# Moving the drive's scaling from TensorE matmuls to GpSimd, and five VectorE steps with it, in a selective-scan block

## The reference, cut to what matters

```python
h   = layernorm(x)                                   # residual of the block
xz  = h @ W_in + b_in;  x_in, z = split(xz)          # 2 x 256 channels
xc  = silu(causal_conv4(x_in) + conv_b)
B, C = split(xc @ W_xp + b_xp)                       # 16 states each, per token
delta = softplus(xc @ W_dt + b_dt)
for s in range(16):                                  # scan over the 256 tokens
    state[s] = exp(delta * A[s]) * state[s] + (delta * xc) * B[s]   # "drive" = u * B[s]
    y += state[s] * C[s]
y   = (y + D_skip * xc) * silu(z)                    # "gate"
r   = h + y @ W_out + b_out
r   = alpha * (r - mean(r)) / (std(r) + eps) + beta  # "alpha, beta"
x1  = x + layernorm(r)                               # "residual sum"
x2  = x1 + layernorm(fp8(layernorm(x1)) @ fp8(W).T + bias)
```

## Time and profile before

| | us |
|---|---|
| runs: median (lowest to highest) | 679.10 (677.97 to 680.75) |
| the profiled execution's own time | 680.76 |
| its span | 679.0 |
| busy in the span: TensorE, VectorE, ScalarE, GpSimd | 559.0, 576.2, 416.4, 322.5 |
| mean granted TensorE clock | 0.909 of full |

### The profile page before, as it was taken

One profiled execution on the slowest core, in us unless ns is written; L12 is line 12 of the kernel. 1 busy time (PEld: TensorE's weight loads), 2 busy tenths in 40 slices (PEclk: granted clock), 3 DMA queues, 4 the chain that ended last, 5 costly groups with the idle time before them and its releaser, 6 DMA issues.

```text
span 679.0 us, 10276 instructions
## 1 busy us (share of the span) xinstructions
PE 559.0 (82%) x2893; PEld 429.9 (63%) x2893; DVE 576.2 (85%) x1106; ACT 416.4 (61%) x814; POOL 322.5 (47%) x331
## 2 busy tenths in 40 slices
PE   4889999997999799986999699979997887773371
PEld 3467787775777577775777567767776776662120
DVE  4057898899998989899989998999989998985595
ACT  2447875785667757776478457765777654621364
POOL 3033554545555536455454654553655545431264
PEclk7979999997999899998999799989999899987555
DMA  7000000000000000000000000000000000000012
GB/s 208 9 1 1 0 1 1 1 0 1 1 1 1 0 2 0 0 0 0 0 0 0 0 1 0 0 0 0 0 0 0 1 1 0 1 1 0 0 47 77
DMA packets 9959, 6.20 MB, mean 9 GB/s; under 512 B 2624, under 2 KB 8896, under 8 KB 9920
## 3 DMA queue, kind: packets, MB, share of 16 engines
q1 hardware_dynamic: 9920, 5.78, 3.1%
HBM read 3.68 MB, written 2.10 MB: 9 GB/s over the span
## 4 chain that ended last, share of the span: by engine, by line
PE 42%; DVE 33%; issue 14%; ACT 5%; POOL 4%; DVEq 1%; DMA 0%; POOLq 0%; ACTq 0%
PE drive L951 16%; DVE state L1162 12%; PE hT L967 8%; PE fbank L894 7%; DVE acc_d L1185 4%; PE fbank L910 2%; PE bbank L985 2%; DVE delta L1145 2%; DVE acc_d L1182 2%; DVE yv L1191 1%; PE drive L894 1%; DVE yg L1196 1%; DVE bst L1205 1%; POOL state L592 1%; ACT h L622 1%
## 5 line engine op out<-in xcount | busy, mean ns | idle before, releaser
L1162 DVE TENSOR_TENSOR_SCAN state<-decay,drive 128x512 f32<-128x512 f32 x256 | 297.1, 1201 | 19.4 <-PE drive L951 18.2
L951 PE MATMUL drive<-diag,uT 128*128 128x256 f32 x1024 | 253.4, 392 | 1.6 <-DVE state L1162 1.0
L951 PEld LDWEIGHTS drive<-diag,uT 128*128 128x128 f32 x1024 | 193.2, 199 | 29.1 <-issue 3.3
L711 ACT ACTIVATE decay<-delta,a_neg 128x510 f32<-128x510 f32 x256 | 169.5, 723 | 20.3 <-DVE state L1162 19.2
L967 PE MATMUL hT<-ident,state 128*128 128x128 f32 x1024 | 147.4, 284 | 36.6 <-DVE acc_d L1185 35.3
L967 PEld LDWEIGHTS hT<-ident,state 128*128 128x128 f32 x1024 | 122.6, 147 | 67.5 <-issue 51.6
L729 ACT ACTIVATE term<-hT,Ct 128x256 f32<-128x256 f32 x256 | 102.6, 478 | 55.3 <-PE hT L967 55.3
L497 POOL TENSOR_SCALAR_AFFINE_SELECT diag<-Bt 128x512 f32<-128x512 f32 x128 | 98.1, 776 | 61.4 <-PE drive L951 40.8
L1185 DVE SCALAR_TENSOR_TENSOR acc_d<-hT,Ct,acc_d 128x256 f32<-128x256 f32 x224 | 92.2, 467 | 0.9 <-PE hT L967 0.9
L512 POOL TENSOR_TENSOR acc<-acc,term 128x512 f32<-128x512 f32 x48 | 61.1, 1272 | 46.6 <-ACT term L729 46.6
L527 POOL TENSOR_TENSOR bstd<-bvar,minus_half 128x4 f32<-128x4 f32 x16 | 16.3, 1017 | 107.2 <-DVE bvar L1253 62.6
(11 more groups left out here) (165 smaller groups left out, 613.3 us busy)
## 6 DMA issues: line engine op xcount, KB each, us to landing
out_dram<-state SPq DMA_DIRECT2D x8, 256.0 KB, 2.2
x_all<-in_L_attn_x_dram SPq DMA_DIRECT2D x2, 256.0 KB, 4.5
state<-in_L_attn_conv_w_dram SPq DMA_DIRECT2D x1, 512.0 KB, 5.8
w_in<-in_L_attn_W_in_dram SPq DMA_DIRECT2D x1, 256.0 KB, 3.1
w_dt<-in_L_attn_W_dt_dram SPq DMA_DIRECT2D x1, 256.0 KB, 5.0
w_out<-in_L_attn_W_out_dram SPq DMA_DIRECT2D x1, 128.0 KB, 3.5
w_ffn<-in_L_ffn_weight_dram SPq DMA_DIRECT2D x1, 64.0 KB, 2.6
bout_r<-in_L_attn_b_out_dram SPq DMA_DIRECT2D x1, 64.0 KB, 3.3
```

Source lines behind the costliest of these rows:

```text
L711: last = nc.scalar.activation(decay[:, g % DECAYS, h, :, s, 1:], delta[:, par, h, :, 1:], ACT.Exp, scale=a_neg[:, h, SG * g + s:SG * g + s ...
L951: last = nc.tensor.matmul(dst[:, :, P * c:P * c + P], uT[:, par, TC * b + c, P * h:P * h + P], diag[:, n % DIAGS, c, :, :], start=True, st ...
L1162: nc.vector.tensor_tensor_scan(state[:, n % STATES, h, :, :].rearrange("p s t -> p (s t)"), decay[:, g % DECAYS, h, b, :, :].rearrange("p ...
```

## The change

The drive is made another way: GpSimd scales the token-major `uT` by B, one tensor_scalar of 128x256 for each chunk and state with B as a scalar for each partition (`scale_b`), into `scaled`; TensorE then only transposes it, eight 128x128 transposes a unit. `front_u`, `back_gate`, alpha and beta, and the residual sum go from VectorE to GpSimd (for the last pair they stay on VectorE); `back_h2T` goes to ScalarE. `TERMS` goes from 4 to 2, `LAG_A` from 3 to 4, and the four step tables are new.

```diff
-LAG_T, LAG_C, LAG_A = 2, 3, 3
+LAG_T, LAG_C, LAG_A = 2, 3, 4
-DECAYS, DIAGS, STATES, TERMS = 2, 4, 4, 4
+DECAYS, SCALED, STATES, TERMS = 2, 4, 4, 2
-POOL_STEPS = dict(front_root=(0,), front_residual=(19,), sum_states=(8,), back_root=(15, 21, 26))
-ACT_STEPS = dict(front_xin=(5, 10), silu_table=(21,), front_silu=(21, 22, 23), exp_table=(23,),
-                 front_norm=(16,), front_xnT=(23,), front_dt=(29, 30), front_exp=(35,), front_log=(35,),
-                 front_uT=(42, 46), back_norms=(33, 41, 47))
-PE_STEPS = dict(front_in=(3, 6, 15, 21), front_transpose=(23,), front_dt=(24, 29), front_bc=(36,),
-                front_ut=(40, 42), back_y=(14, 17), back_out=(20,), back_transpose=(46,))
-DVE_STEPS = dict(front_stats=(1,), front_shift=(2,), front_low=(21,), front_bc=(25,), front_delta=(24,),
-                 front_u=(25,), back_y=(9, 11), back_gate=(11,), back_norms=(11, 13, 17, 21, 24, 27, 27),
-                 back_amax=(30,), back_h2T=(31,))
+POOL_STEPS = dict(front_root=(1,), front_residual=(13,), front_u=(23,), back_gate=(10,), back_affine=(20,),
+                  back_sum=(23,), sum_states=(4,), back_root=(14, 22, 26))
+ACT_STEPS = dict(back_h2T=(47,), front_xin=(8, 12), silu_table=(21,), front_silu=(21, 22, 23), exp_table=(23,),
+                 front_norm=(19,), front_xnT=(23,), front_dt=(29, 33), front_exp=(34,), front_log=(36,),
+                 front_uT=(44, 44), back_norms=(33, 42, 47))
+PE_STEPS = dict(front_in=(0, 5, 16, 19), front_transpose=(22,), front_dt=(24, 28), front_bc=(32,),
+                front_ut=(38, 41), back_y=(14, 15), back_out=(18,), back_transpose=(47,))
+DVE_STEPS = dict(front_stats=(0,), front_shift=(1,), front_low=(19,), front_bc=(21,), front_delta=(23,),
+                 back_y=(9, 10), back_norms=(13, 13, 15, 21, 23, 27, 28), back_amax=(31,))
...
-            def diag_b(pr, par, n):
+            def scale_b(pr, par, n):
                 g, b = n // PAIR, n % PAIR
                 if n == 0:
                     pool.wait_ge(bc_ready, nth(pr, 3, 2))
+                    pool.wait_ge(uT_ready, nth(pr, 2, 2))
-                old = trailing(pr, par, n, DIAGS)
+                old = trailing(pr, par, n, SCALED)
                 if old:
                     pool.wait_ge(drive_ready, nth(old[0], 2 * UNITS, 2 * old[2] + 2))
...
-                nc.gpsimd.affine_select(out=diag[:, n % DIAGS, :, :, :].rearrange("p c s t -> p (c s) t"), in_=b_cols,
-                                        compare_op=ALU.is_equal, fill=0.0, base=0, pattern=[[0, TC * SG], [-1, P]],
-                                        channel_multiplier=1).then_inc(diag_ready, 1)
+                for c in range(TC):
+                    for s in range(SG):
+                        last = nc.gpsimd.tensor_scalar(scaled[:, n % SCALED, c, s, :], uT[:, par, TC * b + c, :],
+                                                       Bt[:, par, g, b, c, s:s + 1], None, ALU.mult)
+                last.then_inc(scaled_ready, 1)
...
+            def front_u(pr, par):
+                pool.wait_ge(delta_ready, nth(pr, 1, 1))
+                nc.gpsimd.tensor_tensor(u[:, :, :], d, xc[:, par, :, :], ALU.mult).then_inc(u_ready, 1)
+            def back_gate(pr, par):
+                pool.wait_ge(y_ready, nth(pr, 2, 2))
+                nc.gpsimd.tensor_tensor(yg[:, :, :], yv[:, :, :], sz[:, par, :, :], ALU.mult).then_inc(gated, 1)
+            def back_affine(pr):
+                pool.wait_ge(b_normed, nth(pr, 2, 1))
+                nc.gpsimd.tensor_tensor(chunks(nrm[:, :]), chunks(nrm[:, :]), on_chunks(alpha_r[:, :]), ALU.mult)\
+                    .then_inc(b_affine, 1)
+                pool.wait_ge(b_affine, nth(pr, 2, 1))
+                nc.gpsimd.tensor_tensor(chunks(nrm[:, :]), chunks(nrm[:, :]), on_chunks(beta_r[:, :]), ALU.add)\
+                    .then_inc(b_affine, 1)
+            def back_sum(pr):
+                pool.wait_ge(b_normed, nth(pr, 2, 2))
+                nc.gpsimd.tensor_tensor(x1, x1, nrm[:, :], ALU.add).then_inc(b_sum, 1)
...
             def drive_unit(pr, par, n):
-                if n == 0:
-                    pe.wait_ge(uT_ready, nth(pr, 2, 2))
-                pe.wait_ge(diag_ready, nth(pr, UNITS, n + 1))
+                pe.wait_ge(scaled_ready, nth(pr, UNITS, n + 1))
...
                     for c in range(TC):
-                        last = nc.tensor.matmul(dst[:, :, P * c:P * c + P], uT[:, par, TC * b + c, P * h:P * h + P],
-                                                diag[:, n % DIAGS, c, :, :], start=True, stop=True)
+                        for s in range(SG):
+                            last = nc.tensor.transpose(drive[:, n % 2, h, L * s + P * c:L * s + P * c + P],
+                                                       scaled[:, n % SCALED, c, s, P * h:P * h + P], ident[:, :])
...
+            def back_h2T(pr):                         # on ScalarE
+                act.wait_ge(back_full, nth(pr, 4, 4))
+                nc.scalar.activation(h2T[:, bass.ds(pr.v * TOK, TOK)], back_bank(pr, 3), ACT.Copy).then_inc(h2T_ready, 1)
```

More of the change, by code:

```diff
@@ L212, in build_sandwich @@
         decay = sb("decay", [P, DECAYS, HALVES, PAIR, SG, L])
-        diag = sb("diag", [P, DIAGS, TC, SG, P])
+        scaled = sb("scaled", [P, SCALED, TC, SG, DI])
         state = sb("state", [P, STATES, HALVES, SG, L])
@@ L328, in build_sandwich @@
         b_root = sem("b_root")
+        b_sum = sem("b_sum")
+        b_affine = sem("b_affine")
         b_shift = sem("b_shift")
@@ L537, in steps_at @@
                         front_residual(nxt, npar)
+                    for _ in due(POOL_STEPS, "front_u", at):
+                        front_u(nxt, npar)
                 if back:
@@ L540, in steps_at @@
                         sum_states(prv, ppar)
+                    for _ in due(POOL_STEPS, "back_gate", at):
+                        back_gate(prv, ppar)
+                    for _ in due(POOL_STEPS, "back_affine", at):
+                        back_affine(prv)
+                    for _ in due(POOL_STEPS, "back_sum", at):
+                        back_sum(prv)
                     for k in due(POOL_STEPS, "back_root", at):
@@ L546, in slot @@
                     if units == UNITS and n + LEAD < units:
-                        diag_b(pr, par, n + LEAD)
+                        scale_b(pr, par, n + LEAD)
                     elif front:
-                        diag_b(pr.plus(1), 1 - par, n + LEAD - units)
+                        scale_b(pr.plus(1), 1 - par, n + LEAD - units)
                     steps_at(pr, par, 2 * n, front, back)
@@ L574, in _ @@
             front_root(Pair(1))
+            front_residual(Pair(0), 0)
+            front_u(Pair(0), 0)
             for n in range(LEAD):
-                diag_b(Pair(0), 0, n)
-            front_residual(Pair(0), 0)
+                scale_b(Pair(0), 0, n)
             slot(Pair(0), 0, True, False)
@@ L696, in front_uT @@
                 act.wait_ge(front_full, nth(pr, 9, 8 + k))
+                if pr.after(2):
+                    act.wait_ge(scaled_ready, nth(pr.plus(-1), UNITS, 0))
                 nc.scalar.activation(uT[:, par, 2 * k:2 * k + 2, :],
@@ L763, in steps_at @@
                         back_norms(prv, k)
+                    for _ in due(ACT_STEPS, "back_h2T", at):
+                        back_h2T(prv)
             def slot(pr, par, front, back, units=UNITS):
@@ L1145, in front_delta @@
                 nc.vector.tensor_tensor(d, dt_v[:, :, :], dt_e[:, :, :], ALU.max).then_inc(delta_ready, 1)
-            def front_u(pr, par):
-                dve.wait_ge(delta_ready, nth(pr, 1, 1))
-                d = delta[:, par, :, :, :].rearrange("p h b t -> p h (b t)")
-                nc.vector.tensor_tensor(u[:, :, :], d, xc[:, par, :, :], ALU.mult).then_inc(u_ready, 1)
             def scan_half(pr, par, n, h):
@@ L1260, in back_sum @@
             def back_sum(pr, par):
[L1262 to L1265 removed]
+                if is_last(pr):
+                    dve.wait_ge(b_normed, nth(pr, 2, 2))
+                    x1 = x_all[:, bass.ds(pr.v * TOK, TOK)]
+                    nc.vector.tensor_tensor(x1, x1, nrm[:, :], ALU.add).then_inc(b_sum, 1)
+                dve.wait_ge(b_sum, nth(pr, 1, 1))
                 dve.sem_inc(dve_waited, 1)
[L1267 removed]
+                stats_of(pr, lambda j: x_all[:, bass.ds(pr.v * TOK + DM * j, DM)], 6)
                 nc.vector.tensor_scalar(bvar[:, :], bmv[:, :, 1], LN_EPS, None, ALU.add).then_inc(b_var, 1)
@@ L1302, in steps_at @@
                         front_delta(nxt, npar)
-                    for _ in due(DVE_STEPS, "front_u", at):
-                        front_u(nxt, npar)
                 if back:
@@ L1307, in steps_at @@
                         back_y(prv, ppar, h)
-                    for _ in due(DVE_STEPS, "back_gate", at):
-                        back_gate(prv, ppar)
                     for k in due(DVE_STEPS, "back_norms", at):
@@ L1313, in steps_at @@
                         back_amax(prv)
```

(3 more changed lines are left out.)

31 lines of the change are left out of this document (13 added, 18 removed).

## The result

The changed kernel takes 846.3 us in the median, against 678.5 before: a ratio of 1.246, with a 95% interval of 1.242 to 1.250. The forecast was 639 us, with 622 to 690 as its range. One run of four took 1119 us, far from the other three (845.5 to 846.8); nothing here explains it, and it is left out of this. The profiled execution took 846.8 us with a span of 844.9.

A forecast was written before the change was run, and what follows sets the result against it. VectorE bounds the kernel now; after the change GpSimd (62.6 us a slot) and VectorE (61.8) nearly tie. Savings 34 (six slots) + 6.5 (slot 0) + 4 (last slot) - 3 (prologue) = 41.5; 680.8 - 41.5 = 639.3, forecast 639, range 622 to 690.

The forecast's parts named there:

- T: Time of one 256-element tensor_scalar in GpSimd's scaling: taken as 0.45 us, from 0.26 to 0.75; 64 a slot make 28.8.
- GpSimd, the open price: Prediction's section on GpSimd's load a slot: 37.7 us today, 62.6 after the change, from 50.4 to 81.8.
- The rest of GpSimd's sum: GpSimd's slot load without scaling: 25.4 us left after losing diag, plus five moved elementwise steps, together 33.8 us.
- Rival 2: GpSimd's scaling dearer still, so TensorE and VectorE wait for `scaled`: slower, 726 us at 0.65 a piece, 775 at 0.75; chance 0.14.
- VectorE's sum: VectorE's busy time in a looped slot falls from 66.9 to 61.8 us, as 5.13 us of steps leave it.
- TensorE's: TensorE's busy time a slot falls from 64.5 to 50.9 us, a unit's drive from 1.89 to 1.04.
- The walk through a slot: One slot followed through all queues: closed at 65 us, plus 1.5 for meetings, 66.5 a slot.
- The ends of the program: Outside the looped slots: prologue 3 us more, last slot 4 less, tail unchanged.
- Rival 1: GpSimd's scaling piece costs 0.49 to 0.56 us and GpSimd is the bound, still faster: 654 to 677 us; chance 0.19.
- Rival 3: TensorE's clock stays down under transposes: 5 us more a slot, about 715 us; chance 0.03.
- Rival 4: u's handover through the engines before a slot's first drive ends 6 us late, gain gone: 679 us; chance 0.07.
- The lock between VectorE and GpSimd: Two-input SBUF instructions of VectorE exclude GpSimd's: some 3 us of waiting a slot inside VectorE's busy time, left unchanged.

The follow-up runs named there:

- half-scaled kernel: Changed kernel with only the first of a unit's two states scaled, the second slice filled with 0.5 once in the prologue; 648.5 us.
- moves alone: Changed kernel with the drive undone (diag by affine_select and matmuls as before), the moved steps and new step tables kept; 653.3 us, ratio 0.960 to the kernel before.
- copy kernel: Changed kernel with a GpSimd tensor_copy of 256 elements in place of each scaling tensor_scalar, B left out of the drive; 636.3 us.
- drive alone: Kernel before with only the drive changed (tensor_scalar scaling on GpSimd, transposes on TensorE) and two term buffers; elementwise steps and tables as before; 815.5 us.
- mixed kernel: Changed kernel with drives by turns: even units tensor_tensor scaling and transposes, odd units affine_select diag and matmuls; 652.4 us, ratio 0.959.

## Why the prediction was wrong, and where it was right

**The step that failed** is the price of T, in "GpSimd, the open price". It took T = 0.45 from affine_select, as the nearest one-input instruction, and 0.75 from the two-input adds as the upper bound. Measured: 0.93 (0.91 from start to start), so 64 of them are 58 us a slot where the sum had 28.8. Both ends rested on one idea, that the number of inputs sets GpSimd's rate. The runs show that the operation sets it: at 256 elements a copy takes 0.40, a tensor_scalar 0.86 with a constant and 0.93 with a scalar for each partition, and a tensor_tensor of 512 with a broadcast input 1.05, less than a tensor_scalar of 512 with 1.57. The bound "above" was no bound. The sentence "Against: there is only one input" put weight where there was none.

**The rest of GpSimd's sum** held. Its load without the scaling was put at 33.8 us; 91.5 less 64 x 0.907 is 33.4. Rival 2 named the mechanism and its place, and with 0.907 in its own formula gives 33.8 + 58.0 + 2.5 = 94.3 for the slot; it was 92.5. It had a chance of 0.14, and its price ended at T = 0.75 and 775 us, so 846 lay outside even that rival, in the 0.03 left for something slower still.

**VectorE's sum** held: 61.8 forecast, 62.0 measured. **TensorE's** held where the scaling did not hold it up: 1.04 us for a unit's drive at the full clock, and 52.4 us busy a slot in the half-scaled kernel for the 50.9 forecast. In the changed kernel it was 58, at the lower clock.

**The walk through a slot** held. With half the scaling, the slot was 67.1 for 66.5; with copies at 0.40, 65.9. That alpha and beta would be the tightest place shows in the half-scaled kernel, where VectorE waited 9.6 us for beta in six slots, the largest of its waits. GpSimd waited 2.1 us a slot for `delta` there, as walked. The stall at `back_res` came to 0.2 us in all six slots; the walk had left it 0.5 in each. Not as walked: scans waited for a drive up to 1.0 us, 7.5 in all in those six slots, where no wait over 0.3 was forecast.

**The ends of the program** were mis-sized. In the half-scaled kernel the span fell by 32.3: 30.6 in the six slots (forecast 34), 4.1 ahead of the first uT copy (forecast 3.5), and behind the last copy it rose by 2.4 where 4 less were forecast. Split at the end of the last scan, that last part is a last slot that fell by 1.6 and a tail that rose by 4.0, where the prediction had 4 less and "The tail is unchanged". In the moves alone the last slot fell by 4.5 and the tail rose by 3.3; in the copy kernel by 3.9 and 4.6. So the tail is what the prediction had wrong in all three, and in the half-scaled kernel the last slot as well. The gate comes 7.9 us behind the last scan in the kernel before, 11.5 in the half-scaled kernel and 11.1 with the moves alone.

It is not GpSimd's adds. The last of them ended at 573.6 in the half-scaled kernel, and VectorE took up the sum at 576.5, behind its own direct sums, which had waited for transposes of TensorE, and these for ScalarE:

```profile
568.89 0.60 ACT L776 ACTIVATE h2T<-bbank 128x512 f32<-128x512 f32 x1 [0.75 <-PE bbank L1040]
569.38 1.56 ACT L769 ACTIVATE term<-hT,Ct 128x256 f32<-128x256 f32 x4
570.36 1.76 PE L1011 MATMUL hT<-ident,state 128*128 128x128 f32 x8 [1.51 <-ACT term L769]
572.37 1.27 POOL L524 TENSOR_TENSOR acc<-acc,term 128x512 f32<-128x512 f32 x1
576.53 1.29 DVE L1423 TENSOR_TENSOR ysumT<-acc,acc_d 128x512 f32<-128x512 f32 x2
```

The term that TensorE waits for stands behind the moved `back_h2T`. Nor is it the later adds and two term buffers: with four buffers and the old distance the tail rose as well, by 4.5. That the place of `back_h2T` is the cause is read from these rows; no run undoes that move alone.

**Rival 1** (0.49 to 0.56, still faster) did not occur, though the tensor_tensor form comes near it: 1.02 us for 512 from start to start is 0.51 for 256, and it took 667 us, inside the 654 to 677 of that rival.

**Rival 3** (the clock stays down) falls. With all drives made by transposes the granted clock in the slots was 0.91 (half-scaled) and 0.89 (copies), in the stretch from 140 to 540 us; in the same stretch it was 0.95 in the kernel before and 0.97 with the moves alone, which keep the matmuls. In the half-scaled kernel one can see what is missing to 1.00. The clock was full from 322 to 352 us; then TensorE waited 4.96 us for u. After that it ran transposes alone (of u, drive and states), first at 0.50 and then at 1.00. The timeline, and then TensorE in stretches as in the earlier trace rows:

```profile
358.71 1.11 PE L981 MATMUL fbank<-ident,u 128*128 128x128 f32 x4 [4.96 <-POOL u L494]
359.61 1.91 PE L995 MATMUL drive<-ident,scaled 128*128 128x128 f32 x8
...
363.15 1.04 PE L995 MATMUL drive<-ident,scaled 128*128 128x128 f32 x8
```

```profile
361.00:362.00 1.00, 1.00 (x7) 0.50 0.00 0
363.00:364.00 1.00, 1.00 (x11) 1.00 0.00 0
```

The clock was at 0.80 to 0.85 only where GpSimd's scaling holds all up (the changed kernel, the runs with a constant, with 512 elements and with the drive alone); in the changed kernel TensorE idles for up to 10.7 us at a time. By the Trainium skill (TensorE: Matmul & The Clock Gate, Part 4) transposes would not engage the full clock; these rows disagree.

**Rival 4** (the handover of u) is part of every wait in the changed kernel, but as a result: TensorE waits 10 us a slot for u because GpSimd stands behind by then. With the moves alone the wait for u was 2.8 us a slot, and moving u back gained nothing that can be told there.

**The lock between VectorE and GpSimd**, kept at 3 us a slot, was right for the changed and the half-scaled kernel by VectorE's total, but not by its parts: `delta` fell from 2.09 to 1.20, since GpSimd now waits for it, while small instructions rose. Where GpSimd ran tensor_tensor in place of tensor_scalar, VectorE's load went up to 65.3 us a slot from 60.5.

## What to carry to other kernels

Price an instruction on GpSimd by a row of the same operation, not by its number of inputs. When no row has it, the honest upper bound is not the next dearer thing in the trace; give the case beyond it a share that shows in the range, or do not multiply the guess by 64. And when an engine is asked to take several jobs, split them: here the same edit held a gain of 4% (the moves alone) and a loss of 20% (the drive alone) that hid it. What a move is worth depends on which engine is the bound: these moves gained 27 us with GpSimd idle a third of the slot, and cost 31 with it full.

## What the runs showed of the hardware

- GpSimd, fp32 in SBUF, 128 partitions: copy of 256 elements 0.40 us; tensor_scalar 0.93 (256) and 1.57 (512), so 2.48 ns an element and 0.30 us; with a constant in place of a partition scalar 0.08 less; tensor_tensor of 512 with two full inputs 1.27, with one broadcast input 1.05; of 1024 with a step of zero in each input 1.90.
- A VectorE instruction of four elements with one SBUF input, 0.17 us by itself, took 0.99 until a GpSimd tensor_tensor ended. The earlier trace rows had shown this for two inputs only. Five kinds of instructions of four elements took 32.5 us in all in the mixed kernel and 12.9 in the half-scaled one.
- With every drive made by transposes, TensorE's granted clock was 0.91 over a stretch in which it was busy 312 of 400 us; after an idle wait of 4.96 us it rose from 0.50 to 1.00 while TensorE ran transposes alone.
